# Reordering the start of a one-core attention and expert kernel: Q of unit 0 ahead of V, and one conditioning job split differently

## What is computed

```python
# cond: r = x, k = v = side
ek = exp(min(k, 30)); ekv = ek * v
nf, df = forward scans of ekv, ek;  nb, db = backward scans
euk = exp(min(u + k, 30))
num = nf + nb - ekv + euk * v
den = df + db - ek + euk
h = sigmoid(r) * (num / max(den, 1e-8)) * (0.8 + 0.2 * tf)
# attention
q, k, v = h @ Wq, h @ Wk, h @ Wv
bias = sigmoid(q @ Wg) * (v @ Wd)
p = softmax(where(causal & (bias > 0), scale * q @ k.T + bias, min))
x = x + (p @ v) @ Wo
```

## Time and profile before

| | |
|---|---|
| median of 3 runs | 564.47 us (563.94 to 565.36) |
| the profiled execution's own time | 562.55 us |
| its span | 560.8 us |
| TensorE, VectorE, ScalarE, GpSimd busy | 86%, 63%, 59%, 43% of the span |
| mean granted TensorE clock | 0.942 of full |
| slices of 14 us with TensorE's granted clock under 0.8 | 42 to 56 us (0.6) and two at the end of the attention, two at the very end |

### The profile page before, as it was taken

One profiled execution on the slowest core, in us unless ns is written; L12 is line 12 of the kernel. 1 busy time (PEld: TensorE's weight loads), 2 busy tenths in 40 slices (PEclk: granted clock), 3 DMA queues, 4 the chain that ended last, 5 costly groups with the idle time before them and its releaser, 6 DMA issues.

```text
span 560.8 us, 10404 instructions
## 1 busy us (share of the span) xinstructions
PE 482.8 (86%) x2771; PEld 400.9 (71%) x2771; DVE 353.6 (63%) x1182; ACT 332.4 (59%) x1022; POOL 241.4 (43%) x255
## 2 busy tenths in 40 slices
PE   0975699999989999999998527999999999999476
PEld 0445577787777867888866425899999999999354
DVE  4757857748567488678688435666666666666144
ACT  3372676789676788887996422555555555555200
POOL 1144301002011543001673777667767666766500
PEclk9996889999998999999999756999999999999779
DMA  8920495200030211300293234999999999992096
GB/s 284 421 80 1 138 330 165 72 1 1 0 78 1 73 43 39 77 2 0 78 336 144 105 105 139 323 402 398 399 396 386 386 395 397 397 390 83 23 399 253
DMA packets 65064, 108.54 MB, mean 194 GB/s; under 512 B 10266, under 2 KB 41191, under 8 KB 64496
## 3 DMA queue, kind: packets, MB, share of 16 engines
q1 hardware_dynamic: 54688, 86.73, 43.6%
q0 software_dynamic: 9168, 16.95, 8.2%
q10 hardware_dynamic: 1152, 4.19, 1.9%
HBM read 81.31 MB, written 34.77 MB: 207 GB/s over the span
## 4 chain that ended last, share of the span: by engine, by line
PE 63%; DVE 11%; ACT 9%; DMA 8%; issue 4%; POOL 4%; ACTq 1%; SPq 0%; POOLq 0%; DVEq 0%
PE ps L1309 14%; PE ps L1329 10%; PE ps L1081 10%; PE ps L1205 6%; DMA pairs<-pair_rows 4%; PE ps L1077 3%; PE ps L1079 3%; PE ps L1078 3%; PE ps L1126 3%; POOL slot_rows L447 2%; PE ps L1159 2%; ACT lg L531 2%; PE ps L1119 2%; ACT lg L588 2%; PE ps L1186 2%
## 5 line engine op out<-in xcount | busy, mean ns | idle before, releaser
L517 POOL DMA_INDIRECT pair_rows<-eout,dest x127 | 124.9, 984 | 56.8 <-DVE dest L1049 46.1
L1309 PE MATMUL ps<-wts,xg 128*128 128x192 f32 x508 | 106.2, 333 | 0.0
L1309 PEld LDWEIGHTS ps<-wts,xg 128*128 128x128 f32 x508 | 81.7, 194 | 0.1
L708 ACT ACTIVATE sact<-ps 128x96 f32<-128x96 f32 x127 | 31.8, 250 | 75.6 <-PE ps L1309 75.1
L1329 PE MATMUL ps<-wts,aT 96*128 96x256 f32 x254 | 76.4, 382 | 0.0
L1046 DVE COPY xg<-ps 128x256 f32<-128x256 f32 x127 | 53.9, 424 | 29.9 <-PE ps L1081 29.4
L588 ACT ACTIVATE lg<-lg,mneg 128x128 f32<-128x128 f32 (+1 forms) x128 | 56.4, 442 | 26.7 <-DVE mneg L844 26.7
L1059 DVE SCALAR_TENSOR_TENSOR aact<-sact,xrow,ps 128x96 f32<-128x96 f32 x127 | 39.8, 314 | 48.3 <-ACT sact L708 47.2
L447 POOL DMA_INDIRECT slot_rows<-rows,pair_slot x48 | 48.1, 1002 | 40.1 <-DVE hit L909 27.4
L531 ACT ACTIVATE eout<-ps 128x256 f32<-128x256 f32 x127 | 48.6, 383 | 17.7 <-PE ps L1329 1.6
L1205 PE MATMUL ps<-oT,wo_sb 128*128 128x256 f32 x256 | 58.0, 379 | 0.7 <-ACT oT L531 0.7
(11 more groups left out here) (197 smaller groups left out, 1058.9 us busy)
## 6 DMA issues: line engine op xcount, KB each, us to landing
wts<-in_experts_dram SPq DMA_DIRECT2D x127, 320.0 KB, 9.3
xrow<-slot_rows SPq DMA_DIRECT2D x127, 130.0 KB, 8.9
slot_rows<-zero SPq DMA_DIRECT2D x1, 8320.0 KB, 29.6
pairs<-pair_rows SPq DMA_DIRECT2D x8, 512.0 KB, 5.1
pairs<-pair_rows ACTq DMA_DIRECT2D x8, 512.0 KB, 21.0
wT<-in_wq_t_dram SPq DMA_DIRECT2D x1, 2048.0 KB, 9.1
wq_raw<-in_wq_l_dram SPq DMA_DIRECT2D x1, 2048.0 KB, 18.0
wo_sb<-in_wo_l_dram SPq DMA_DIRECT2D x1, 2048.0 KB, 17.7
```

Of the source, the lines that this page charges most:

```text
L517: nc.gpsimd.indirect_dma_start(out=pair_d, out_offset=bass.IndirectOffsetOnAxis(ap=dest[:, t:t + 1], axis=0), in_=eout[t % NOUT][:], in_of ...
L1309: ins = nc.tensor.matmul(ps[:, 2 + u % 2, 0:I2], xg[u % 3][:, cc, :], wts[u % NBUF][:, cc * I2:(cc + 1) * I2], start=(cc == 0), stop=(cc = ...
```

## The change

It changes only the order in the four compute queues:

- In `first_projs`, the two Q halves of unit 0 come ahead of the two V halves; TensorE makes the scores of unit 0 after six projections instead of eight.
- ScalarE copies piece 0 of Wq's high part before the first evictions, and pieces 1 to 3 after the exponentials of job (0,1), ahead of softmax_exp(0); V and Q of unit 1 are evicted after it.
- GpSimd does the masks of batch 0 before the low parts 1 to 3, and no longer waits for the bias; its sums of job (0,1) come after all low parts.
- VectorE takes the Q low parts before the scans of job (0,1), makes the logits of unit 0 right after part 1, and does part 2 after V's and Q's low parts.
- Parts 3 and 4 of job (0,1) go into round 0; job (0,2) runs one part later in rounds 0 to 2, with two late parts in round 2. ScalarE copies `hh` always at the end of a round.
- cond_sums adds the denominator first, and part 3 waits for that add alone, part 4 for both.

```diff
-        first_projs = [("G", 0, 0), ("K", 0, 0), ("K", 0, 1), ("B", 0, 0), ("V", 0, 0), ("V", 0, 1),
-                       ("Q", 0, 0), ("Q", 0, 1), ("Q", 1, 0), ("Q", 1, 1)]
+        first_projs = [("G", 0, 0), ("K", 0, 0), ("K", 0, 1), ("B", 0, 0), ("Q", 0, 0), ("Q", 0, 1),
+                       ("V", 0, 0), ("V", 0, 1), ("Q", 1, 0), ("Q", 1, 1)]
...
         def round_parts(u):
-
+            if u == 0:
+                return [(0, 1, 3), (0, 1, 4)], [(0, 2, 0)]
+            if u < 3:
+                return round_jobs[2 * u - 1:2 * u], round_jobs[2 * u:2 * u + 1 + u // 2]
             return round_jobs[2 * u:2 * u + 1], round_jobs[2 * u + 1:2 * u + 2]
...
+                nc.gpsimd.tensor_tensor(df[:], df[:], euk[:], ALU.add).then_inc(cond_sum, 1)
                 nc.gpsimd.tensor_tensor(nf[:], nf[:], eukv[:], ALU.add).then_inc(cond_sum, 1)
-                nc.gpsimd.tensor_tensor(df[:], df[:], euk[:], ALU.add).then_inc(cond_sum, 1)
...
             cond_products((0, 1))
-            pool.wait_ge(bias_ready, 1)
-            wq_low(1)
-            wq_low(2)
             masks(0)
+            for n in range(1, KV):
+                wq_low(n)
             cond_sums((0, 1))
-            wq_low(3)
...
-            for j in first_projs[:4]:
+            wq_high(0)
+            for j in first_projs[:6]:
                 proj_hi_part(j)
-            wq_high(0)
-            for j in first_projs[4:6]:
-                proj_hi_part(j)
-            wq_high(1)
             cond_exps((0, 1))
-            for j in first_projs[6:8]:
-                proj_hi_part(j)
-            wq_high(2)
-            wq_high(3)
+            for n in range(1, KV):
+                wq_high(n)
             softmax_exp(0)
-            for j in first_projs[8:]:
+            for j in first_projs[6:]:
                 proj_hi_part(j)
             normalise(0)
             softmax_exp(1)
-            h_hi_part(1)
...
-                    dve.wait_ge(cond_sum, 2 * (n + 1))
+                    dve.wait_ge(cond_sum, 2 * n + 1)
...
                 else:
+                    dve.wait_ge(cond_sum, 2 * (n + 1))
...
             cond_part(0, 1, 1)
-            for j in first_projs[6:8]:
+            make_logits(0)
+            for j in first_projs[6:]:
                 proj_lo_part(j)
-            make_logits(0)
             cond_part(0, 1, 2)
-            for j in first_projs[8:]:
-                proj_lo_part(j)
             row_sums(0)
             make_logits(1)
-            cond_part(0, 1, 3)
-            cond_part(0, 1, 4)
-            h_lo_part(1)
...
-            for j in first_projs[:8]:
+            for j in first_projs[:6]:
                 proj(j)
             make_scores(0)
-            for j in first_projs[8:]:
+            for j in first_projs[6:]:
                 proj(j)
             make_scores(1)
```

More of the change, by code:

```diff
@@ L664, in _ @@
                         cond_exps((c, jb))
-                    if part == 4 and c == 0:
-                        h_hi_part(jb)
                 for b in routed(u, 0):
@@ L686, in _ @@
                         cond_exps((c, jb))
+                for c, jb, part in early + late:
                     if part == 4 and c == 0:
```

## The result

| | before | changed |
|---|---|---|
| median of the timed runs | 564.47 us (11 runs, 562.08 to 565.36) | 568.24 us (11 runs, 565.67 to 570.78) |
| ratio | | 1.0071, 95% interval 1.0052 to 1.0089 |
| the profiled execution's span | 560.8 us | 566.5 us |
| mean granted TensorE clock | 0.942 | 0.940 |

The account below looks back on a forecast made before the run. TensorE, busy 86% of the span, was taken as the bound, so late delays are paid in full. 1.34 + 1.64 - 0.7 + 0.15 + 1.3 = +3.7 us gave 568.2 us on the timed runs' scale, range 562.5 to 571.0.

Parts of the forecast that it names:

- part 5: Round 0, end of job (0,1): G of batch 1 waits for `hf`, +1.34 us, and TensorE's lowered clock costs +1.64.
- Part 1: Gate eviction: `ge` caught behind POOL's low part of Wq for 2.39 us, delaying the chain to the last `kl` by 1.3.
- Parts 2 and 3: Q of unit 0 ahead of V, masks and scans by turns: scores at 37.9, logits of unit 0 at 45.5, 5.8 us early.
- Part 4: Ahead of round 0: V eviction behind the softmax, then exposed part 2, leave 1.6 us of 5.8; first `pt` at 67.6.
- Part 6: Job (0,2) a part later in rounds 1 and 2: -0.7, +0.15 and +1.3 us; the swap of sums gains nothing.
- From round 3 on the jobs stand as before ... nothing: Rounds from 3 on: jobs stand as before and the swapped sums meet the same collision, so no change in time.
- the likeliest case: The forecast itself for the whole kernel: 568.2 us, 567 to 569.5 for this case alone, chance 0.50.
- clock stays up over the wait: Faster rival: collisions spared, TensorE's clock stays up over round 0's wait for `hf`, clamp not held; -2.1 us, 562.4, chance 0.11.
- half absorbed: Rival: only one collision is spared, or slack in rounds 1 to 3 takes up part; +1.5 us, 566.0, chance 0.17.
- collisions spared: Rival: `ge` isn't caught and the last scan slips ahead of `wql`; sum +0.6 us, time 565.1, chance 0.15.

Follow-up runs that it names:

- c_ge: Changed kernel with POOL's first low part of Wq held until the bias is ready; ratio to the kernel before 1.0107.
- r_parts34: Changed kernel with parts 3 and 4 of job (0,1) back ahead of round 0 and job (0,2) in its old rounds; ratio to before 1.0013.
- e_order: r_parts34's program with V of batch 0 evicted before unit 0's exponentials, its low part before the logits, part 2 right behind them; ratio to before 0.9873.
- f_order: e_order with unit 1's Q halves also evicted before the exponentials; their low parts, unit 1's logits and unit 0's row sums before part 2; ratio to before 0.988.
- b_part2: Changed kernel with part 2 of job (0,1) taken right behind the logits of unit 0; ratio to before 1.007.
- d2_clock: Changed kernel with four extra 128x512 matmuls, later overwritten, ahead of TensorE's wait for `hf` before G of batch 1; ratio to before 1.0109.
- r_after: The changed kernel run once more, unaltered, on another chip; ratio to before 1.0162.
- s_swap: Changed kernel with the numerator summed first again and part 3 waiting for both sums; one timed execution, 621.31 us.
- h_before: Kernel before, with only the copy of `hh` of jobs (0,2) and (0,3) moved to the end of their round; ratio to before 1.0014.

## Why the prediction was right, and where only its total was

568.2 us were predicted and 568.24 measured. The cause and the place are shown, but that the total is as close as that is luck: part 5 was 2.2 us too small, and the 1.5 us that round 7 gives back were not in the sum.

- **Part 1, `ge` caught by the low part: right.** 2.34 us against 2.39, 0.03 us behind POOL's start. c_ge shows that the collision is POOL's doing. The 1.3 us that I gave the step are what it costs at the upper level of the clock, as r_parts34, e_order and f_order show (`kl` 6.84 or 6.85 us after the zero, 5.55 before). In the changed kernel's first profile the level fell over the K projection, and there K came last anyway: `kl` at 7.49, and with `ge` free in c_ge still at 7.22.
- **Parts 2 and 3: right in the chain.** Scores, turns and the held last scan (2.76 us) came as told. Logits of unit 0 at 46.78, less 0.6 of the zero 46.2, against 45.5. The 0.7 are the K projection's clock, which I had taken as full: in r_parts34, the same order with the upper level there, they start 19.55 us after the zero, 45.5 on the scale of before.
- **Part 4: right.** Idle VectorE ahead of V's low part, part 2 from 57.90, row sums at 61.96 (60.9 predicted, on a zero 0.6 earlier), first `pt` 68.1 on the scale of before against 67.6. Of the early gain of 5.8 us 1.1 were left, not 1.6. b_part2 and e_order show the structure behind it: part 2 alone can't be moved to much advantage (0.6 us), part 2 and V's eviction together can (5.5 to 6.1 us).
- **Part 5: the mechanism right, both terms too small.** The wait for `hf` was put at +1.34 and is +2.56 (G at 51.08 against 48.52 after the zero): 0.5 from the first `pt`; 0.6 from the Q low parts of unit 2, behind which the clamp starts 3.52 us after the first `pt` copy and not 2.95; and 0.2 in the chain from the clamp to G, 5.47 us and not 5.3. The clock was put at +1.64, between 0 and 2, by the row of the 2.79 us hole. It is +2.64 in the trace, and d2_clock took 2.5 of it back. The upper bound of 2 was wrong: I took the loss from one place, a hole of 2.79 us with weighing behind it. Here the hole is 3.49 us with G and V behind it, and the level read 0.50 from 77 to 83 us; which of the two differences makes it longer no run separates. Together 2.2 us too little. The length of the wait itself, 3.49 us against 3.5, came out right because both of its ends were late by nearly the same: the weighing ended at 73.6 on the scale of before, and not at 72.3.
- **Part 6: right.** Rounds 1 and 2 add 0.8 us against 0.75. Up to the K projection of round 2, 0.64 us are won (0.17 in r_after), where -0.7 and +0.15 were put: the scan of `bscan` is down from 1.47 to 0.41 us and the wait for `ql` from 1.10 to 0.42. From there to scores(4) 1.46 are lost, where +1.3 was put: the clamp was held by the second sum, as worked out, and `kl` (113.91) then held the scores. The Trainium skill (SBUF — State Buffer, Who interferes with whom) calls the port pair an exclusive lock, held for an instruction, and by it I gave the swap nothing. The trace agrees with the lock (clamp 1.48 us under the sum, 0.42 free; `ge` 2.34 against 0.17). But the inference from it was off by 0.6 us: s_swap shows that without the swap the clamp runs into the next holder.
- **"From round 3 on the jobs stand as before ... nothing": wrong.** The copy of `hh` was followed into round 0 only. ScalarE's wait for `hf` of job (0,3), 1.88 us in round 7 of the kernel before, I hadn't looked up, and its removal gives 1.5 us back. h_before shows it alone.

So the sum was 3.7, and its terms as measured are 5.2 + 0.8 - 1.5 = 4.5, with the timed 3.8 (2.9 to 5.0) around both. The range of the likeliest case, 567 to 569.5, held too. The rival "clock stays up over the wait" was refuted by both profiles of the changed kernel; "half absorbed" (+1.5) and "collisions spared" (+0.6) lie outside the interval, and in the profiles both collisions are there.

## What to carry to other kernels

An early gain counts only if the next shared resource is free at the earlier time: follow the edit up to the first wait of the bounding engine, and there price the wait and what the engine's clock may lose behind it, which here was the same size again (2.6 us each). When an instruction is moved for all rounds, look at it in every round, since the one that pays may not be the one that you are reading. Work that fills a hole of another engine (here 4.2 us in VectorE's queue before the first `pt`) must not be moved behind the event that ends the hole.

## What the runs showed of the hardware

- An operation of VectorE on 128x8 elements, 0.17 us alone, is held for as long as POOL's 128x1024 subtraction runs: 2.34 or 2.35 us in all eleven profiles in which the subtraction started 0.02 to 0.03 us earlier. The masks hold a scan for less (1.05 us) than the product (1.67) or `wql` (2.73 to 2.77).
- Behind the wait for `hf`, 3.49 us (4.51 in b_part2), TensorE's clock stayed at its lower level through the whole of the two projections, 5.25 us instead of 2.61, in five profiles out of five. Four 128x512 products put into the wait, 3.60 us, kept it up.
- A wait of that length did not bring the clock down every time: behind 3.25 us between project_out(5) and (6) it stayed up in f_order, while behind 3.15 to 3.55 us in the other thirteen profiles the stretch took 1.4 to 4.3 us longer at a mean clock of 0.92 to 0.79.
- Over the K projection near 28 us the same program had the upper level in one execution and the lower in the next, twice. It was 1.00 in both executions with the old order ahead of round 0; whether that order protects it, two executions can't tell.
